# Low-rank and gating product of the feed-forward pass with high and low weight columns side by side

## What is computed

```python
x = layernorm(x + attention(x, wq, wk, wv, wo))      # causal, 32 heads of 32, 8 key heads
# feed-forward, xf = x as [4096, 1024]
h = xf @ gw1.T + gb1                                 # 32 gating features
h = (h - mean(h)) * rsqrt(var(h) + 1e-5) * ln_gamma + ln_beta
gates = relu(h) @ gw2.T + gb2                        # 8 experts
top_v, top_i = top_k(gates, 2); top_g = softmax(top_v)
w = ... # weight of each expert per token; experts over their capacity get 0
main = xf @ weight.T
tmp = einsum('ni,eir->enr', xf, lora_A) * w.T[:, :, None]   # 8 experts, rank 16: 128 low-rank features
out = main + einsum('enr,ero->no', tmp, lora_B) / 16
x = layernorm(x + out)
```

## Time and profile before

| | |
|---|---|
| median of three runs | 3563.53 us (3563.51 to 3566.39) |
| the profiled execution | 3560.88 us, its span 3559.1 us |
| PE busy | 3456.3 us (97%), 25818 matmuls |
| PEld busy | 2440.5 us (69%) |
| DVE busy | 1977.8 us (56%) |
| ACT busy | 1468.6 us (41%) |
| POOL busy | 1633.2 us (46%) |
| DMA | 340.67 MB, mean 96 GB/s |
| granted TensorE clock | mean 0.988 |

### The profile page before, as it was taken

How to read it: one execution, slowest core, us unless ns; L and a number is a source line. 1 busy time by engine, 2 the same in 40 slices (tenths; PEclk the granted TensorE clock), 3 DMA queues, 4 the chain that set the end, 5 groups by cost and what they waited for, 6 DMA issues and landing times. The chain is left out here.

```text
span 3559.1 us, 62842 instructions
## 1 busy us (share of the span) xinstructions
PE 3456.3 (97%) x25818; PEld 2440.5 (69%) x25818; DVE 1977.8 (56%) x3577; ACT 1468.6 (41%) x1839; POOL 1633.2 (46%) x702
## 2 busy tenths in 40 slices
PE   8999998999999999999999999999959999999999
PEld 7888885666666666666666666666538888888887
DVE  3121116777667677677767767777525666542222
ACT  3111112555555555555556555555542222221111
POOL 0000003877887798797788779879330000000000
PEclk9999997999999999999999999999989999999999
DMA  6344325021111111112111111110037877755553
GB/s 213 113 124 119 117 90 119 24 54 49 34 42 49 43 31 51 48 34 51 49 34 42 49 48 28 49 40 8 11 108 219 233 222 226 207 195 177 179 174 128
DMA packets 248223, 340.67 MB, mean 96 GB/s; under 512 B 55440, under 2 KB 150288, under 8 KB 247952
## 3 DMA queue, kind: packets, MB, share of 16 engines
q1 hardware_dynamic: 247952, 336.87, 32.1%
HBM read 203.08 MB, written 133.17 MB: 94 GB/s over the span
## 5 line engine op out<-in xcount | busy, mean ns | idle before, releaser
L684 DVE TENSOR_REDUCE p_part_max<-p_qm 128x1 f32<-128x512 f32 (+3 forms) x2240 | 1407.7, 671 | 597.4 <-PE p_qm L534 342.4
L504 POOL TENSOR_TENSOR p_psums<-p_psums,p_probs 128x1024 f32<-128x1024 f32 x575 | 1369.0, 2381 | 87.3 <-ACT p_probs L643 2.8
L647 ACT ACTIVATE p_probs<-p_km 128x1024 f32<-128x1024 f32 x896 | 879.8, 1022 | 480.7 <-PE p_km L562 404.5
L534 PE MATMUL p_qm<-p_k_st,p_q_st 96*128 96x512 f32 (+3 forms) x2560 | 912.8, 420 | 12.3 <-DMA p_q_st<-q_hi 10.8
L534 PEld LDWEIGHTS p_qm<-p_k_st,p_q_st 96*128 96x128 f32 x2560 | 480.9, 194 | 253.8 <-issue 112.6
L562 PE MATMUL p_km<-p_q_st,p_k_st 97*128 97x512 f32 x1792 | 599.6, 416 | 14.7 <-ACT p_probs L647 9.6
L569 PE MATMUL p_o<-p_probs,p_v 128*32 128x256 f32 (+1 forms) x9216 | 569.8, 371 | 0.0
L500 POOL TENSOR_TENSOR p_psums<-p_probs 128x1024 f32<-128x1024 f32 x110 | 262.2, 2384 | 353.8 <-ACT p_probs L647 353.8
L569 PEld LDWEIGHTS p_o<-p_probs,p_v 128*32 128x32 f32 x9216 | 270.6, 110 | 216.0 <-issue 44.2
L562 PEld LDWEIGHTS p_km<-p_q_st,p_k_st 97*128 97x128 f32 x1792 | 311.7, 191 | 114.3 <-ACT p_probs L647 70.9
L41 PE MATMUL p_acc<-p_xT_hi,p_w_hi 128*128 128x512 f32 x640 | 250.4, 391 | 9.7 <-DVE p_w_lo L226 9.7
(11 more groups left out here) (150 smaller groups left out, 4129.5 us busy)
## 6 DMA issues: line engine op xcount, KB each, us to landing
p_q_st<-q_hi SPq DMA_DIRECT2D x128, 256.0 KB, 4.7
p_x_raw<-in_xT SPq DMA_DIRECT2D x64, 256.0 KB, 3.5
q_hi<-p_out_hi SPq DMA_DIRECT2D x64, 256.0 KB, 2.0
q_lo<-p_out_lo SPq DMA_DIRECT2D x64, 256.0 KB, 2.3
p_q_st<-q_lo SPq DMA_DIRECT2D x64, 256.0 KB, 4.4
attended_T<-p_o_raw SPq DMA_DIRECT2D x128, 128.0 KB
p_a_raw<-attended_T SPq DMA_DIRECT2D x32, 512.0 KB, 5.2
p_recip<-reciprocals SPq DMA_DIRECT2D x128, 128.0 KB, 6.7
```

Source lines behind the costliest of these rows:

```text
L504: pool.tensor_tensor(sums[:, :, :], sums[:, :, :], probs[s % PB][:, :, :], ALU.add).then_inc(added, 1)
L534: last = pe.matmul(bank[:, x * keys:(x + 1) * keys], q_st[par][0:ROWS, c, h + x, sub * P:(sub + 1) * P], k_st[par][0:ROWS, j * CK:j * CK + ...
L647: act.activation(tile[:, :, :].rearrange("p h q -> p (h q)"), km[s % 2][:, :, :].rearrange("p a b -> p (a b)"), ACT.Exp, scale=SCALE).then ...
L684: dve.reduce_max(part_max[c][:, h:h + heads, sub, j], qm[bank_of(i)][:, 0:item_width(i)].rearrange("p (h k) -> p h k", h=heads), AX.X).the ...
```

## The change

The high and low parts of the 160 weight columns, two arrays before, become one array of 2 x 160 columns for each slice of 128 features: ag_w. Instead of three matmuls of 160 columns, PE does one of 320 columns with yT_hi (high x high into columns 0 to 159 of the bank, high x low into columns 160 to 319) and one of 160 columns with yT_lo and the high columns (added into columns 0 to 159). ACT's `keep_low` is replaced by `copy_part`, which copies columns 160 to 319 to SBUF (part) and raises part_copied. DVE's `hidden` first adds part to columns 0 to 159 and writes the 160 sums to low, which has grown to 160 columns, and raises low_done; then it adds the bias to columns 128 to 159 of low. So low_done is now raised by DVE, and PE's wait for h_done is dropped. The store of low takes the first 128 of its 160 columns.

```diff
@@ -742,7 +742,7 @@
         eps = sb("p3_eps", [P, 1])
         experts = sb("p3_experts", [P, E])
         experts_i = sb("p3_experts_i", [P, E], I32)
-        ag_hi, ag_lo = sb("p3_ag_hi", [P, KC, AG], F32R), sb("p3_ag_lo", [P, KC, AG], F32R)
+        ag_w = sb("p3_ag_w", [P, KC, 2 * AG], F32R)
         gw2T = sb("p3_gw2T", [GH, E])
         rows = sb("p3_rows", [P, ROWS])
         wm_raw = sb("p3_wm_raw", [P, D])
@@ -753,7 +753,8 @@
         a_hi = [sb(f"p3_a_hi{i}", [P, KC, P], F32R) for i in range(2)]
         a_lo = [sb(f"p3_a_lo{i}", [P, KC, P], F32R) for i in range(2)]
         yT_hi, yT_lo = sb("p3_yT_hi", [P, KC, P], F32R), sb("p3_yT_lo", [P, KC, P], F32R)
-        low = [sb(f"p3_low{i}", [P, ER]) for i in range(2)]
+        low = [sb(f"p3_low{i}", [P, AG]) for i in range(2)]
+        part = [sb(f"p3_part{i}", [P, AG]) for i in range(2)]
         stats = sb("p3_stats", [P, 2, 6])
         mean_var = [sb(f"p3_mean_var{i}", [P, 2]) for i in range(2)]
         std = [sb(f"p3_std{i}", [P, 1]) for i in range(2)]
@@ -826,7 +827,8 @@
         yT_hi_done, yT_lo_done = sem("p3_yT_hi_done"), sem("p3_yT_lo_done")
         y_stored = [sem(f"p3_y_stored{i}") for i in range(2)]
         yT_stored = sem("p3_yT_stored")
-        ag_done, low_done, h_done = sem("p3_ag_done"), sem("p3_low_done"), sem("p3_h_done")
+        ag_done, part_copied = sem("p3_ag_done"), sem("p3_part_copied")
+        low_done, h_done = sem("p3_low_done"), sem("p3_h_done")
         low_stored = [sem(f"p3_low_stored{i}") for i in range(2)]
         g_var_done, g_std_done, hid_done = sem("p3_g_var_done"), sem("p3_g_std_done"), sem("p3_hid_done")
         hidT_ps_done, hidT_done = sem("p3_hidT_ps_done"), sem("p3_hidT_done")
@@ -912,7 +914,7 @@
                 if 3 <= t:
                     u = t - 3
                     sp.wait_ge(low_done, u + 1)
-                    sp.dma_start(low_d[u, :, :], low[u % 2][:, :]).then_inc(low_stored[u % 2], 16)
+                    sp.dma_start(low_d[u, :, :], low[u % 2][:, 0:ER]).then_inc(low_stored[u % 2], 16)
                 if 1 <= t and t + 1 < NT:
                     sp.wait_ge(sum_done, t)
                     load_x(t + 1)
@@ -998,11 +1000,10 @@
                     pe.wait_ge(ag_lo_done, 1)
                 else:
                     pe.wait_ge(low_done, t)
-                    pe.wait_ge(h_done, t)
                 pe.wait_ge(yT_lo_done, t + 1)
                 for k in range(KC):
-                    last = matmul3(pe, ag_ps[:, 0:AG], yT_hi[:, k, :], yT_lo[:, k, :],
-                                   ag_hi[:, k, :], ag_lo[:, k, :], k == 0, k == KC - 1)
+                    pe.matmul(ag_ps[:, 0:2 * AG], yT_hi[:, k, :], ag_w[:, k, :], start=k == 0, stop=False)
+                    last = pe.matmul(ag_ps[:, 0:AG], yT_lo[:, k, :], ag_w[:, k, 0:AG], start=False, stop=k == KC - 1)
                 last.then_inc(ag_done, 1)
 
             def turn_hidden(t):
@@ -1118,11 +1119,11 @@
                 act.activation(yT_hi[:, :, :].rearrange("p k t -> p (k t)"),
                                tr_ps[:, :, :].rearrange("p a b -> p (a b)"), ACT.Copy).then_inc(yT_hi_done, 1)
 
-            def keep_low(t):
+            def copy_part(t):
                 act.wait_ge(ag_done, t + 1)
                 if t >= 2:
-                    act.wait_ge(low_stored[t % 2], 16 * (t // 2))
-                act.activation(low[t % 2][:, :], ag_ps[:, 0:ER], ACT.Copy).then_inc(low_done, 1)
+                    act.wait_ge(low_done, t - 1)
+                act.activation(part[t % 2][:, :], ag_ps[:, AG:2 * AG], ACT.Copy).then_inc(part_copied, 1)
 
             def copy_hidden(t):
                 act.wait_ge(hidT_ps_done, t + 1)
@@ -1153,7 +1154,7 @@
                 if 2 <= t < NT + 2:
                     split_yT(t - 2)
                 if 3 <= t < NT + 3:
-                    keep_low(t - 3)
+                    copy_part(t - 3)
                 if 4 <= t < NT + 4:
                     copy_hidden(t - 4)
                 if 1 <= t <= NT:
@@ -1188,7 +1189,7 @@
             for n in range(3, KC):
                 split_wo(n)
             act.wait_ge(ag_in, 16)
-            act.activation(ag_hi[:, :, :], ag_raw, ACT.Copy).then_inc(ag_hi_done, 1)
+            act.activation(ag_w[:, :, 0:AG], ag_raw, ACT.Copy).then_inc(ag_hi_done, 1)
             for t in range(NT + 2):
                 step(t)
             act.wait_ge(lb_in, 16)
@@ -1263,10 +1264,13 @@
             def hidden(t):
                 h = hid[t % 2]
                 dve.wait_ge(ag_done, t + 1)
+                dve.wait_ge(part_copied, t + 1)
+                if t >= 2:
+                    dve.wait_ge(low_stored[t % 2], 16 * (t // 2))
+                    dve.wait_ge(hidT_ps_done, t - 1)
+                dve.tensor_tensor(low[t % 2][:, :], ag_ps[:, 0:AG], part[t % 2][:, :], ALU.add).then_inc(low_done, 1)
                 dve.wait_ge(low_done, t + 1)
-                if t >= 2:
-                    dve.wait_ge(hidT_ps_done, t - 1)
-                dve.tensor_tensor(h[:, :], ag_ps[:, ER:AG], gb1_b, ALU.add).then_inc(h_done, 1)
+                dve.tensor_tensor(h[:, :], low[t % 2][:, ER:AG], gb1_b, ALU.add).then_inc(h_done, 1)
                 dve.wait_ge(h_done, t + 1)
                 chain.link(dve.bn_stats(g_stats[:, 0, :], h[:, :]))
                 dve.bn_aggr(g_mean_var[:, :], g_stats[:, :, :]).then_inc(g_var_done, 1)
@@ -1357,7 +1361,8 @@
                 split_wo(n)
             reciprocals(1)
             dve.wait_ge(ag_hi_done, 1)
-            dve.tensor_tensor(ag_lo[:, :, :], ag_raw, ag_hi[:, :, :].bitcast(F32), ALU.subtract).then_inc(ag_lo_done, 1)
+            dve.tensor_tensor(ag_w[:, :, AG:2 * AG], ag_raw, ag_w[:, :, 0:AG].bitcast(F32), ALU.subtract
+                              ).then_inc(ag_lo_done, 1)
             dve.wait_ge(small_in, 32)
             dve.wait_ge(experts_done, 1)
             for t in range(NT + 3):
```

## The result

The changed kernel takes 3627.2 us (median of four runs, 3624.1 to 3632.0) against 3563.5 before (3562.8 to 3566.4): 63.7 us more, a ratio of 1.018 with a 95% interval of 1.016 to 1.020. The forecast was 3631, the range 3590 to 3662. The profiled execution took 3624.14 us with a span of 3622.4, 63.3 us over that of before.

What follows compares the result with a forecast made beforehand. PE bounds the kernel before at 15.18 us per tile; the change closes a 17.7 us loop through DVE and DMA. 68.5 us later at the last output projection, less 1, is 67.5; plus 3563.5 gives 3631.0 us, range 3590 to 3662.

Steps and rivals of the forecast that it cites:

- PE's product: Low-rank and gating product on PE: eight pairs at 0.147 + 0.112 us, 2.07 us per tile instead of 2.73.
- The release: low_done on DVE, raised 1.5 us after the division's start: 1.14 to the next instruction plus 0.34 for the addition.
- The link: Division, low_done, transfers, reciprocals landed, next division: 1.5 plus 16.2 us, 17.7 per link, bounds 16.6 to 18.6.
- Where the loop starts and ends: Feed-forward pass: 27 links from step 3's division at 2709.34; last output projection 5.1 us after step 30's division, 68.5 later.
- The tail: After the last output projection starts: three shortened products gain 2.0 us, second pass's late first loads cost about 1 us.
- The waits that I had called covered: yT_hi's wait for yT's store hidden behind 11 us of matmuls; product's low_done wait of 1 to 2 us inside the loop.
- The first (the loop hides): Loop short enough to hide, PE stays the bound at 14.5 us per tile: 3543 us; chance 8%.
- The second (16.3 us): Loop binds but the transfer phases close up, links of 16.3 us: 3593 us; chance 14%.
- The third, the clock: PE's idle time drops its clock for half of a tile's work, 21.8 us per tile: 3742 us; chance 5%.
- The fourth, landings that come 3 us late: DMA landings 3 us late in one of five tiles are paid in full: 3647 us; chance 8%.
- The fifth, no visible change: 320 column matmul at 0.23 us and a loop that just fits: 3563 us; chance 2%.
- The estimate from the Trainium skill: 2.0 us plus bytes over 436 GB/s: 9.4 us for a tile's 3.2 MB, link 10.9; the trace showed 16.

Runs made afterwards that it cites:

- The control: The kernel before, with the wait for low_done and the store of low moved to the end of SP's step: 3562.8 us, ratio 1.000.

## Why the prediction was right, point by point

- *PE's product.* Predicted 0.147 + 0.112 us per pair, 2.07 per tile; measured 0.26 per pair. The sum was right; the split was not, since the matmul of 160 columns behind one of 320 steps by 0.07 (2903.82 to 2903.89) and the 320 wide one by 0.19.
- *The release.* Predicted 1.5 us behind the division, measured 1.49; the addition took 0.32 us (0.34).
- *The link.* Predicted 16.2 us from low's issue to the division, measured 2903.28 to 2919.50 = 16.2 in the link shown, and 17.52 - 1.49 = 16.03 in the mean. The link of 17.7 was 0.18 us too long, 5.0 us over 27 links. That is the largest error of the sum. The prediction put the slow reciprocals down to small packets; that isn't it, as a_raw runs at 310 GB/s in packets of the same 512 bytes.
- *Where the loop starts and ends.* The division of step 3 came at 2707.06, not at 2709.34: nothing ahead of it waits for low_done. Of the 2.3 us, 0.9 are there at the first division of the pass (2646.23 against 2647.11); the rest wasn't traced. PE's last output projection started at 3184.99, that is 4.99 us behind the last division (5.1 predicted), and 61.2 us later than before (68.5 predicted; 5.0 of the difference are the links, 2.3 the start).
- *The tail.* Predicted 1 us gained: 2 by three shorter products, less 1 for late first loads of the second pass. Measured, from the start of that output projection to the end of the span: 3622.4 - 3184.99 = 437.4 us against 3559.1 - 3123.83 = 435.3 before, 2.1 us lost. The products gave what was forecast: with the store of low last, the same stretch takes 3547.0 - 3113.54 = 433.5 us, 1.8 less than before. The late first loads were the mis-sized part, 4 us instead of 1. PE stood idle for 2.02 us ahead of the second pass, and there the clock fell, a cost that the sum did not have: the first 24 matmuls of that pass took 7.3 us (3201.80 to 3209.06), against 5.7 with the store last. Where only the release moved, no clock fell there, and the stretch took 1.0 us more than before (436.3). The term was wrong by 3 us in the other direction than the links, and so it is in part luck that the total came within 4 us.
- *The waits that I had called covered.* yT_hi waits for the store of yT, 174 us in 28 times. It costs nothing: DVE's low part of yT, which follows it, stands ahead of the division, and the division still waited 4.5 to 7.7 us for the reciprocals in each of the 27 links. PE's waits of 1.11 and 1.07 us in a tile lie inside the loop (2.2 together, where the prediction had 3): with the loop opened at the store of low the first is left once (2.1 us, at the start of the pass) and the second once (0.18 us), without a change to PE or DVE.
- *The rivals.* The first (the loop hides) is what the kernels with half of the reciprocals and with the one wide transfer show: it needed a link under 14.55 us, and the transfers of this kernel are too slow for it. The second (16.3 us) is refuted by 17.52. The third, the clock, was right about the fall and wrong about its price: the prediction called a granted clock under 1 in this pass a sign against itself, and it came, in 4 of 27 links, but PE's longer tile there still fitted into the loop. The fourth, landings that come 3 us late, did not occur: the longest link is 1.5 us above the mean. The fifth, no visible change, is refuted by an interval of 1.016 to 1.020.
- *The estimate from the Trainium skill.* The prediction took 9.4 us for a step's bytes from the Trainium skill, "DMA: Bandwidth & Descriptors", section "Anatomy of one DMA — SWDGE (gpsimd) path". The way from low's issue to the division is 16.0 us here in the mean. The Trainium skill gives this fit there for one DMA on the gpsimd path, and here SP issues ten in a row; of the 6.6 us between the two, 4.8 are the reciprocals, which took 6 us where that rate of the Trainium skill gives an estimated 1.2.

## What to carry to other kernels

A signal has a place in its raiser's order, and a list of transfers has a place for its wait; when a change moves a signal from one engine to another, ask what the new raiser does ahead of it, and what stands behind the wait in the queue. If the answers meet, as here in the reciprocals' landing, a loop has been closed, and its length is the sum of all its parts however much every engine idles. The wait for a late signal belongs behind the transfers that do not need it: moved there, the same change is worth 17 us, and at 3546 us it is faster than both kernels. The control says what such a move is worth by itself: nothing, as long as the signal comes early.

## What the runs showed of the hardware

- Four transfers of 128 KB, each reading one row for 32 partitions, flowed at 73 GB/s; with 32 different rows, of another array, at 210; and 512 KB in one transfer to 128 partitions, in packets of the same 512 bytes, close to the 310 GB/s of a_raw. The whole phase was 6, 4 and 2 us.
- The first large transfer of a burst, a load of 512 KB, ran near 200 GB/s, the three stores behind it at 380 to 426. Loads of wo ran at 414 to 430.
- A matmul of 160 columns in a row of its like stepped by 0.11 us; between two of 320 it stepped by 0.07 and these by 0.19.
- The granted clock fell from 1.00 to 0.50 in 4 of the 27 links and once behind the pass, each time within 2 us of the end of an idle stretch of TensorE of 1.66 to 2.59 us; behind the last one the first 24 matmuls of 512 columns took 7.3 us instead of 5.7.
